# Second image of a linear-attention layer: fewer filter taps on TensorE, output projections placed between its filter sets, and denominators placed ahead of the last key-value product

## The chip, the cores and the metric

The kernel runs on one core of one Trainium2 chip. The metric is the device time of one launch in microseconds. Before the change the median of three runs is 846.25 us (844.39 to 847.61).

The engines are named as in the profile: PE is TensorE (matrix products), PEld its loads of weights, DVE is VectorE, ACT is ScalarE, POOL is GpSimd, SP issues transfers. All data of this layer is float32.

## What is computed

Four layers are applied in turn to x of shape (2, 256, 32, 32), each as `x = x + layer(groupnorm(x))`. The change is in the third, a linear attention with a local branch. Its reference, cut to what matters (B = 2 images, N = 1024 pixels, 768 channels of q, k and v):

```python
qkv = einsum('bchw,oc->bohw', x, w_qkv)                 # 768 channels
y = conv(qkv, w_dw, 5x5, padding 2, one filter per channel)
y = conv(y, w_pw, 1x1, groups of 8 channels)
mqkv = concatenate([qkv, y], axis=1).reshape(B, -1, 24, N)   # heads of 8 q, 8 k, 8 v
q, k = relu(mqkv[:, :, :8]), relu(mqkv[:, :, 8:16])
v = pad(mqkv[:, :, 16:], one more row of ones)
vk = einsum('bhdn,bhen->bhde', v, k)
out = einsum('bhde,bhen->bhdn', vk, q)
out = out[:, :, :-1] / (out[:, :, -1:] + 1e-15)
out = einsum('bchw,oc->bohw', out.reshape(B, -1, H, W), w_proj)
out = batchnorm(out)
```

So there are two sources: qkv itself (source 0) and the filtered y, the "local" branch (source 1). Each has its own keys, values and queries, and both go into the projection.

## The kernel before

**Tiles.** The 768 channels lie in six tiles t of 128: 0 and 2 are keys, 1 and 3 values, 4 and 5 queries. A **unit** (t, b) is a tile of one image, 128 x 1024 values. `Y_UNITS` lists the twelve units in the order in which TensorE finishes them. For image 0 that is tiles 0, 2, 4, 5, 1, 3 (units 0 to 5 of the list), for image 1 tiles 0, 2, 4, 1, 3, 5 (units 6 to 11).

**The 25 taps of a filter are shared out.** The first `TENSOR_TAPS[t]` taps of a unit run on TensorE, with matrices that hold the filter weight times the 1x1 weights, so that the sum lands in its final place. One tap of one unit is a **set**: four matmuls of 64 x 512 in the four corners of the array (`local_set`, L1031). The other taps are summed elsewhere: for tiles 0, 2, 4 and 5 by VectorE, one `scalar_tensor_tensor` of 128 x 1024 per tap with its sum in PSUM banks 6 and 7 (`filter_tap`, L402 for the first, L406 for the rest); for tiles 1 and 3 ScalarE makes the product of each tap (`tap_products`, L1773) in one of four buffers, and GpSimd adds it (L2003 the first, L2006 the rest). `pool_taps` lists these, 19 per unit and 76 in all. TensorE then adds that sum, multiplied by the 1x1 weights, to its own (`local_rest`, four matmuls, L1048), and ScalarE copies the finished unit out (`copy_local`, L1815 to L1819), after which its two banks are free. Units use banks 2, 3 and banks 4, 5 in turn, so the first set of a unit waits until the unit two before it is copied out. `REST_WITHIN` says inside which unit, and before which of its taps, the rest of the unit before is placed; None means that it stands in the written order.

**Keys times values.** For a block n of 128 pixels TensorE transposes keys and values (`key_value_step`, L960), ScalarE copies them out (L1799), and TensorE multiplies them (`key_value_product`, L970). Blocks 0 to 15 are source 0, 16 to 23 source 1 of image 0, 24 to 31 source 1 of image 1. From block 16 on all transposes go through one bank, so each step waits for the copy of the one before. VectorE masks the sum to the heads (`mask_products`, L1422), TensorE multiplies the projection into it (`merge_projection`, L992), ScalarE copies the merged matrix (L1830).

**Queries and output.** TensorE sums the denominators (`denominators`, L983), VectorE inverts them (`invert_denominators`, L1431 and L1432), TensorE spreads the inverses over the channels (`spread_pair`, L1013), VectorE scales the queries (`weigh_queries`, L1438). `project(i, ks)` (L1059) is one block of 128 x 512 of the output: i = 0 to 3 are image 0, 4 to 7 image 1; ks 0 and 1 are source 0, ks 2 and 3 source 1. VectorE adds each block to x (`update_x2`, L1448) and takes moments for the next group normalisation (L1167).

**What sets the order.** Each engine runs its program in order; the interleaving is written out by hand. On TensorE it is the sequence of calls from L1085 on. On VectorE a counter `done` runs over the filter taps, and tables place the other steps after a given tap: `MASK_AT`, `INVERT_AT`, `WEIGH_QUERIES_AT`, `UPDATE_AT`. On ScalarE `PRODUCTS_BEFORE[n]` is the number of tap products made before unit n is copied out. VectorE's units are (0,0), (2,0), (4,0), (5,0), (0,1), (2,1), (4,1), (5,1), with 17 taps each before the change, so taps 102 to 118 are unit (4,1) and 119 to 135 unit (5,1).

Of the kernel before, what the change touches and what calls it, by code (L numbers as in the profile page):

```python
# [37 lines left out]
WT = 8  # L38
TILES = B * WT
# [6 lines left out]
K5 = 25  # L46
TENSOR_TAPS = [8, 6, 8, 6, 8, 8]

HALF = P // 2
QUARTERS = [(0, 0, 0), (1, 0, 1), (0, 1, 1), (1, 1, 0)]  # L50
Y_UNITS = [(t, 0) for t in (0, 2, 4, 5, 1, 3)] + [(t, 1) for t in (0, 2, 4, 1, 3, 5)]
REST_WITHIN = [None, 5, 5, 5, 1, 3, 1, 5, 5, 1, 4, None]
SETS_WITH_KV, SETS_PER_PAIR = 8, 6
WEIGH_AT, WEIGH_LOCAL_AT = 18, 42
MASK_AT = [56, 102]
INVERT_AT = [57, 84]
WEIGH_QUERIES_AT = [61, 66, 71, 76, 87, 90]
UPDATE_AT = [107, 111, 126, 129]
PRODUCTS_BEFORE = [31, 36, 41, 44, 50, 54, 70, 74, 76, 76, 76, 76]

# [49 lines left out]
def mixer_kernel(nc, x_in, out, w, xpad_dram, general_dram):  # L110
    cv_at, cv_n = channel_columns()
    with ExitStack() as ctx:
# [202 lines left out]
        for t in range(QKV_TILES):  # L315
            pwt.append(words(o, TENSOR_TAPS[t] * HALF).rearrange("p (a m) -> p a m", m=HALF))
            o += TENSOR_TAPS[t] * HALF
        projw = words(o, 1024).rearrange("p (k c) -> p k c", k=4); o += 1024
# [29 lines left out]
        def den_bank(part):  # L348
            return 0 if part else 1

# [5 lines left out]

        sets_before = [sum(TENSOR_TAPS[t] for t, b in Y_UNITS[:n]) for n in range(len(Y_UNITS) + 1)]

# [24 lines left out]

        pool_taps = [(t, a, b) for b in range(B) for a in range(TENSOR_TAPS[POOL_TILES[0]], K5) for t in POOL_TILES]
        early_tmp = [local[0][4], local[0][5], spare_tmp]
# [12 lines left out]
        def filter_tap(eng, t, b, a):  # L398

            wt = col("dw2_w", t * K5 + a)  # L400
            if a == TENSOR_TAPS[t]:
                return eng.tensor_scalar(filter_acc, tap_view(t, a, b), wt, None, ALU.mult)  # L402
            dst = filter_acc
            if a == K5 - 1:
                dst = local[b][t].rearrange("p (y x) -> p y x", y=H)
            return eng.scalar_tensor_tensor(dst, tap_view(t, a, b), wt, filter_acc, ALU.mult, ALU.add)  # L406
# [274 lines left out]
        def _(pe):  # L681
# [420 lines left out]
            for i in range(2):  # L1102
                project(i, range(4))
                sets = local_sets(sets, sets + 1)
            sets = local_sets(sets, sets_before[11])
            local_rest(10)
            for i in (2, 3):
                project(i, range(4))

            sets = local_sets(sets, sets + 3)  # L1110
            pe.wait_ge(s_yqe, 11)
            pe.wait_ge(s_x_new, 20)
            for n in range(TILES + WT, 2 * TILES):
                key_value_step(n)
                if sets < sets_before[12]:
                    sets = local_sets(sets, sets + 1)
                if n > TILES + WT:
                    key_value_product(n - 1)
                if n == 2 * TILES - 3:
                    local_rest(11)  # L1120
            key_value_product(2 * TILES - 1)
            merge_projection(3)
            for i in (4, 5):
                project(i, (0, 1))
            pe.wait_ge(s_yqe, 12)
            pe.wait_ge(s_mgc, 4)
            denominators(2)
            for i in (6, 7):
                project(i, (0, 1))
            spread_pair(12)  # L1130
            spread_pair(14)
# [28 lines left out]
        def _(dve):  # L1160
# [294 lines left out]
            for u, (t, b) in enumerate(DVE_UNITS):  # L1455
                dve.wait_ge(s_qp, CHUNKS * Q_ORDER.index(t) + 2 * (b + 1))
                for tap in range(TENSOR_TAPS[t], K5):
                    if tap > TENSOR_TAPS[t]:
                        me.upto(tap_n)
                    elif u:  # L1460
                        dve.wait_ge(s_dwd, u)
# [79 lines left out]
        def _(act):  # L1541
# [305 lines left out]
            for n in range(7, 11):  # L1847
                tap_products(PRODUCTS_BEFORE[n])
                copy_local(n)
            copy_turned(TILES + WT, 2 * TILES, 76)  # L1850
            copy_merged(3)
# [38 lines left out]
        def _(pool):  # L1890
# [84 lines left out]
            def tap_matrices(t):  # L1975
                taps = TENSOR_TAPS[t]
                return g.tensor_tensor(pwt[t], pwm[:, t, :].unsqueeze(1).to_broadcast([P, taps, HALF]),
                                       col("dw2_w", t * K5, taps).unsqueeze(2).to_broadcast([P, taps, HALF]), ALU.mult)
# [12 lines left out]
            for n, (t, tap, b) in enumerate(pool_taps):  # L1991
                if tap == TENSOR_TAPS[t] and b == 1:
                    pool.wait_ge(s_tr, TILES)
                if n == WEIGH_AT:
                    pool.wait_ge(s_qf, CHUNKS * (Q_ORDER.index(2) + 1))
                    denominator_weights(0, 0, 2)
                if n == WEIGH_LOCAL_AT:
                    pool.wait_ge(s_yqe, 2)
                    denominator_weights(1, 0, 1)
                pool.wait_ge(s_tp, n + 1)  # L2000
                dst = local[b][t]
                if tap == TENSOR_TAPS[t]:
                    g.tensor_copy(dst, tap_tmp(n)).then_inc(s_ta, 1)  # L2003
                else:
                    pool.wait_ge(s_ta, n - 1)
                    g.tensor_tensor(dst, dst, tap_tmp(n), ALU.add).then_inc(s_ta, 1)  # L2006
# [161 lines left out]
```

## Time and profile before

| | us |
|---|---|
| median of three runs | 846.25 |
| the profiled execution | 846.58 |
| its span, first to last instruction | 844.9 |
| third layer's filters and attention, first VectorE tap to last projection | 544.8 to 789.0 |
| of it, from image 0's projections on | 703.3 to 789.0 |
| PE busy, share of the span | 692.0 (82%) |
| DVE busy | 559.9 (66%) |
| ACT busy | 330.7 (39%) |
| POOL busy | 350.5 (41%) |

The profiled execution is 0.33 us above the median, and 1.7 us of it lie outside the span. The timelines quoted below have one row per run of like instructions: start in us from the span's start, duration, engine, line, operation, shapes, number of instructions, and in brackets how long the engine had been idle and for what. One fp32 matmul of the code shows as two MATMUL records, so a set is x8 and one `project` over four ks is x8. In a table of stretches PEclk is the granted clock of TensorE as a share of its full 2.4 GHz; 0.50 is 1.2 GHz.

### The profile page before, as it was taken

The numbers are of one execution on the slowest core, as the hardware profiler recorded it, in microseconds if no ns is written. First come the engines' busy times: TensorE is split into PE (matmuls) and PEld (weight loads), VectorE is DVE, ScalarE is ACT, GpSimd is POOL, SyncE is SP. The second block draws the span as 40 slices with busy tenths as digits, with TensorE's granted clock in tenths as the row PEclk, the third lists the DMA queues.
The fourth block names the chain that finished last, engine by engine and source line by source line (L and its number), as shares of the span: only waits on it lengthen the run. The fifth ranks groups of instructions, "written<-read, shape, count | busy, mean of one in ns | idle before, by whom it ended". The sixth has DMA issues, their size and how long they took to land.

```text
span 844.9 us, 8797 instructions
## 1 busy us (share of the span) xinstructions
PE 692.0 (82%) x3446; PEld 376.2 (45%) x3446; DVE 559.9 (66%) x616; ACT 330.7 (39%) x454; POOL 350.5 (41%) x196
## 2 busy tenths in 40 slices
PE   1959346987986799999799999597999988898666
PEld 0656145777983465443211555243533343243222
DVE  6895878993957335301235323699999998762797
ACT  3603680002000433001344111379889867421433
POOL 5620029998650532000000000519999979400260
PEclk9989769999999899999978999798999999899789
DMA  5059100085102713900216300200000000000002
GB/s 177 0 80 153 17 2 1 1 118 97 24 1 73 251 74 144 402 27 1 100 65 209 125 1 0 80 0 1 1 1 1 1 1 2 1 1 1 13 0 99
DMA packets 37622, 49.51 MB, mean 59 GB/s; under 512 B 2628, under 2 KB 25988, under 8 KB 36252
## 3 DMA queue, kind: packets, MB, share of 16 engines
q1 hardware_dynamic: 37580, 48.94, 21.3%
q8 instruction: 27, 0.44, 0.2%
q14 instruction: 15, 0.12, 0.1%
HBM read 28.19 MB, written 10.49 MB: 46 GB/s over the span
## 4 chain that ended last, share of the span: by engine, by line
PE 50%; DVE 29%; POOL 8%; issue 5%; ACT 4%; DMA 3%; SPq 0%; POOLq 0%; DVEq 0%; ACTq 0%
DVE psum L406 14%; PE psum L822 8%; PE psum L760 6%; PE psum L932 3%; PE psum L793 3%; POOL arena L1930 3%; PE psum L1031 3%; PE psum L736 3%; POOL arena L1933 3%; PE psum L1059 2%; PE psum L918 2%; PE psum L896 2%; DVE psum L436 2%; PE psum L1154 2%; PE psum L695 2%
## 5 line engine op out<-in xcount | busy, mean ns | idle before, releaser
L406 DVE SCALAR_TENSOR_TENSOR psum<-arena,psum 128x1024 f32<-128x1024 f32 x120 | 154.6, 1289 | 3.8
L2006 POOL TENSOR_TENSOR arena<-arena 128x1024 f32<-128x1024 f32 x72 | 143.6, 2029 | 11.0 <-ACT arena L1773 10.4
L760 PE MATMUL psum<-arena 128*128 128x128 f32 x800 | 93.6, 277 | 12.9 <-DVE arena L477 8.9
L760 PEld LDWEIGHTS psum<-arena 128*128 128x128 f32 x800 | 88.6, 142 | 17.8 <-DVE arena L477 10.9
L477 DVE TENSOR_TENSOR arena<-arena,psum 128x2048 f32<-128x2048 f32 x38 | 83.9, 2285 | 17.4 <-ACT psum L1673 13.5
L1031 PE MATMUL psum<-arena 64*64 64x512 f32 x704 | 90.0, 627 | 0.9 <-ACT arena L1817 0.9
L1773 ACT ACTIVATE arena<-arena 128x1024 f32<-128x1024 f32 x76 | 87.2, 1179 | 4.5 <-POOL arena L2006 4.5
L1965 POOL MEMSET arena<- 128x864 f32 x1 | 0.8, 836 | 197.1 <-DVE arena L1403 197.1
L822 PE MATMUL psum<-arena 128*128 128x512 f32 x144 | 63.8, 602 | 0.0
L477 POOL TENSOR_TENSOR arena<-arena 128x2048 f32<-128x2048 f32 x12 | 43.6, 3651 | 13.5 <-PE psum L760 13.4
L747 PE MATMUL psum<-arena 128*128 128x128 f32 x162 | 21.4, 294 | 31.2 <-DVE arena L1312 31.2
L947 PE MATMUL psum<-arena 128*128 128x512 f32 x96 | 43.0, 610 | 4.3 <-ACT arena L1569 4.3
L1031 PEld LDWEIGHTS psum<-arena 64*64 64x64 f32 x704 | 24.9, 136 | 47.3 <-issue 47.3
L822 PEld LDWEIGHTS psum<-arena 128*128 128x128 f32 x144 | 27.0, 188 | 36.6 <-issue 36.6
L1357 DVE TENSOR_REDUCE arena<-arena 128x16 f32<-128x496 f32 (+1 forms) x12 | 7.4, 669 | 50.8 <-ACT arena L1722 50.8
L1336 DVE TENSOR_TENSOR arena<-arena 128x512 f32<-128x512 f32 x16 | 12.1, 756 | 38.5 <-ACT arena L1710 38.3
L1669 ACT ACTIVATE arena<-psum 128x512 f32<-128x512 f32 x8 | 4.4, 600 | 83.7 <-PE psum L760 83.7
L747 PEld LDWEIGHTS psum<-arena 128*128 128x128 f32 x162 | 20.4, 208 | 32.7 <-issue 26.4
L1407 DVE TENSOR_TENSOR arena<-arena,psum 128x512 f32<-128x512 f32 x16 | 11.0, 687 | 35.6 <-PE psum L871 35.6
L1059 PE MATMUL psum<-arena 128*128 128x512 f32 x64 | 30.2, 621 | 2.2 <-ACT arena L1830 1.4
L1799 ACT ACTIVATE arena<-psum 128x512 f32<-128x512 f32 x32 | 19.1, 597 | 31.6 <-PE psum L960 31.5
L947 PEld LDWEIGHTS psum<-arena 128*128 128x128 f32 x96 | 18.8, 197 | 27.8 <-issue 22.9
(229 smaller groups left out, 1278.3 us busy)
## 6 DMA issues: line engine op xcount, KB each, us to landing
arena<-fc_w_dram SPq DMA_DIRECT2D x10, 1024.0 KB, 11.9
bounce<-arena SPq DMA_DIRECT2D x32, 256.0 KB, 2.0
arena<-bounce SPq DMA_DIRECT2D x32, 256.0 KB, 5.3
arena<-arena SPq DMA_DIRECT2D x16, 480.0 KB
arena<-x_dram SPq DMA_DIRECT2D x4, 512.0 KB, 5.0
out_dram<-arena SPq DMA_DIRECT2D x4, 512.0 KB, 2.6
arena<-sp_w_dram SPq DMA_DIRECT2D x1, 1152.0 KB
arena<-arena SPq DMA_DIRECT2D x8, 140.0 KB
```

What stands on the lines that cost most here:

```text
L406: return eng.scalar_tensor_tensor(dst, tap_view(t, a, b), wt, filter_acc, ALU.mult, ALU.add)
L477: return eng.tensor_tensor(prods[n % NB].rearrange("p (x g c) -> p x g c", g=GH, c=CG), shifted(hf, j, i), weight, ALU.mult)
L736: m = pe.matmul(psum[:, t % 8, 0:NOM], g1cm[:, k, t, :], omw[:, k], start=(k == 0), stop=(k == 1))
L747: m = pe.matmul(psum[:, bank, at * XG:(at + 1) * XG], ident, wk[n % 2][:, (3 * i + j) * XG:(3 * i + j + 1) * XG], start=(bank not in opene ...
L760: m = pe.matmul(psum[:, 4 * hf + xx // 4, xx % 4 * P:(xx % 4 + 1) * P], prods[n % NB][:, xx * P:(xx + 1) * P], ident, start=(first and xx ...
L793: m = pe.matmul(psum[:, i % 4, :], Zc1[:, 2 * k + b, t::WT], pw1w[:, k], start=(k == 0), stop=(k == 1))
L822: m = pe.matmul(psum[:, c, :], sp1w[:, k, tap], Z[:, 2 * k + b, y0:y0 + 16, PAD - 1 + dx:PAD - 1 + dx + W], start=(k == 0 and tap == 0), s ...
L947: m = pe.matmul(psum[:, i % 4, :], qkvw[:, k, t * P:(t + 1) * P], z2[:, k, c * BANK:(c + 1) * BANK], start=(k == 0), stop=(k == 1))
L1031: pe.matmul(psum[y_rows(to), y_banks(n)[half], :], pwt[t][rows, tap, :], padq[rows, t, b, y0:y0 + 16, dx:dx + W], start=(tap == 0), stop=F ...
L1059: m = pe.matmul(psum[:, proj_bank(i), :], merged[:, src, b, gr, mh * P:(mh + 1) * P], queries(src, b, gr)[:, c * BANK:(c + 1) * BANK], sta ...
L1773: a.activation(tap_tmp(n).rearrange("p (y x) -> p y x", y=H), tap_view(t, tap, b), ACT.Copy, scale=col("dw2_w", t * K5 + tap)).then_inc(s_ ...
L2006: g.tensor_tensor(dst, dst, tap_tmp(n), ALU.add).then_inc(s_ta, 1)
```

## The change

Image 1 gets its own numbers of taps on TensorE: `[8, 4, 8, 4, 8, 5]` in place of `[8, 6, 8, 6, 8, 8]`. That is 37 sets in place of 44. Tiles 1 and 3 of image 1 have 21 taps instead of 19 on ScalarE and GpSimd (80 in all instead of 76), and tile 5 of image 1 has 20 instead of 17 on VectorE (139 taps in all instead of 136). Image 0 and the buffers for the matrices keep their sizes. The tables of VectorE and ScalarE are set anew, two projections of image 0 move in between the sets, the rest of unit 9 moves behind the last set of unit 10, and the end of the layer is reordered. The denominators of image 1 move from bank 0 to bank 7.

```diff
-TENSOR_TAPS = [8, 6, 8, 6, 8, 8]
+TENSOR_TAPS = [[8, 6, 8, 6, 8, 8], [8, 4, 8, 4, 8, 5]]
-REST_WITHIN = [None, 5, 5, 5, 1, 3, 1, 5, 5, 1, 4, None]
+REST_WITHIN = [None, 5, 5, 5, 1, 3, 1, 5, 5, 1, None, None]
-MASK_AT = [56, 102]
+MASK_AT = [56, 105]
-UPDATE_AT = [107, 111, 126, 129]
-PRODUCTS_BEFORE = [31, 36, 41, 44, 50, 54, 70, 74, 76, 76, 76, 76]
+UPDATE_AT = [110, 114, 121, 127]
+PRODUCTS_BEFORE = [31, 36, 41, 44, 50, 54, 70, 74, 78, 80, 80, 80]
...
         def den_bank(part):
-            return 0 if part else 1
+            return (1, 0, 7)[part]
...
             for i in range(2):
                 project(i, range(4))
                 sets = local_sets(sets, sets + 1)
+            sets = local_sets(sets, sets_before[9])
+            project(2, range(4))
+            sets = local_sets(sets, sets_before[10])
+            project(3, range(4))
             sets = local_sets(sets, sets_before[11])
+            local_rest(9)
             local_rest(10)
-            for i in (2, 3):
-                project(i, range(4))
-
-            sets = local_sets(sets, sets + 3)
+
+            sets = local_sets(sets, sets + 2)
             pe.wait_ge(s_yqe, 11)
             pe.wait_ge(s_x_new, 20)
...
+            pe.wait_ge(s_yqe, 12)
+            denominators(2)
             key_value_product(2 * TILES - 1)
-            merge_projection(3)
             for i in (4, 5):
                 project(i, (0, 1))
-            pe.wait_ge(s_yqe, 12)
+            merge_projection(3)
+            project(6, (0, 1))
+            spread_pair(12)
+            project(7, (0, 1))
             pe.wait_ge(s_mgc, 4)
-            denominators(2)
-            for i in (6, 7):
-                project(i, (0, 1))
-            spread_pair(12)
             spread_pair(14)
```

The first place is TensorE from the second projection of image 0 to the first transposes of image 1's local keys and values. L1031 is sets (x4 is one set), L1048 rests, L1059 projections, L960 transposes. Before:

```order
L1059 MATMUL psum<-arena 128x512 x4
L1031 MATMUL psum<-arena 64x512 x20
L1048 MATMUL psum<-arena 64x512 x4
L1031 MATMUL psum<-arena 64x512 x16
L1048 MATMUL psum<-arena 64x512 x4
L1031 MATMUL psum<-arena 64x512 x36
L1048 MATMUL psum<-arena 64x512 x4
L1031 MATMUL psum<-arena 64x512 x8
L1048 MATMUL psum<-arena 64x512 x4
L1059 MATMUL psum<-arena 128x512 x8
L1031 MATMUL psum<-arena 64x512 x12
L960 MATMUL psum<-arena 128x128 x4
```

The same stretch in the changed kernel:

```order
L1031 MATMUL psum<-arena 64x512 x20
L1048 MATMUL psum<-arena 64x512 x4
L1031 MATMUL psum<-arena 64x512 x12
L1059 MATMUL psum<-arena 128x512 x4
L1031 MATMUL psum<-arena 64x512 x4
L1048 MATMUL psum<-arena 64x512 x4
L1031 MATMUL psum<-arena 64x512 x12
L1059 MATMUL psum<-arena 128x512 x4
L1031 MATMUL psum<-arena 64x512 x16
L1048 MATMUL psum<-arena 64x512 x8
L1031 MATMUL psum<-arena 64x512 x8
L960 MATMUL psum<-arena 128x128 x4
```

One projection now stands ahead of the rest of unit 8 (the second L1048) and one behind it, the rests of units 9 and 10 stand together (x8), and 18 sets stand between the projection and the transposes where there were 23.

The second place is the end of the layer on TensorE, from the last transposes to the last projections: L970 are products of keys and values, L983 the denominators, L992 the merge, L1013 the spreading. Before:

```order
L960 MATMUL psum<-arena 128x128 x4
L970 MATMUL psum<-arena 128x128 x4
L992 MATMUL psum<-arena 128x256 x2
L1059 MATMUL psum<-arena 128x512 x4
L983 MATMUL psum<-arena 32x512 x4
L1059 MATMUL psum<-arena 128x512 x4
L1013 MATMUL psum<-arena 128x512 x4
L1059 MATMUL psum<-arena 128x512 x8
```

And in the changed kernel:

```order
L960 MATMUL psum<-arena 128x128 x4
L970 MATMUL psum<-arena 128x128 x2
L983 MATMUL psum<-arena 32x512 x4
L970 MATMUL psum<-arena 128x128 x2
L1059 MATMUL psum<-arena 128x512 x4
L992 MATMUL psum<-arena 128x256 x2
L1059 MATMUL psum<-arena 128x512 x2
L1013 MATMUL psum<-arena 128x512 x2
L1059 MATMUL psum<-arena 128x512 x2
L1013 MATMUL psum<-arena 128x512 x2
L1059 MATMUL psum<-arena 128x512 x8
```

The denominators moved ahead of the last product, the merge behind two half projections, and the other two half projections stand ahead of and between the spreads.

The third place is VectorE at unit (4,1), from its first tap on. L1422 (L1425 in the changed kernel) is the mask, L1448 (L1451) an update of x:

```order
 L402 TENSOR_SCALAR psum<-arena 128x1024
-L1422 TENSOR_TENSOR arena<-psum,arena 128x256
-L406 SCALAR_TENSOR_TENSOR psum<-arena,psum 128x1024 x5
-L1448 SCALAR_TENSOR_TENSOR arena<-psum,arena 128x512
+L406 SCALAR_TENSOR_TENSOR psum<-arena,psum 128x1024 x3
+L1425 TENSOR_TENSOR arena<-psum,arena 128x256
+L406 SCALAR_TENSOR_TENSOR psum<-arena,psum 128x1024 x5
+L1451 SCALAR_TENSOR_TENSOR arena<-psum,arena 128x512
 L406 SCALAR_TENSOR_TENSOR psum<-arena,psum 128x1024 x4
```

Three taps of the unit moved ahead of the mask; the distances from the mask to the first two updates, five and four taps, stayed.

## Rows read from the trace of the kernel before

**Rows 1.** The page's chain that ended last, shares of the span by line:
```profile
DVE psum L406 14%; PE psum L822 8%; PE psum L760 6%; PE psum L932 3%; PE psum L793 3%; POOL arena L1930 3%; PE psum L1031 3%; PE psum L736 3%; POOL arena L1933 3%; PE psum L1059 2%; PE psum L918 2%; PE psum L896 2%; DVE psum L436 2%; PE psum L1154 2%; PE psum L695 2%
```
**Rows 2.** Timeline of DVE, units (4,1) and (5,1) (start, duration, what, idle before):
```profile
700.25 0.42 DVE L1422 TENSOR_TENSOR arena<-psum,arena 128x256 f32<-128x256 f32 x1 [4.26 <-PE psum L970]
...
714.96 7.90 DVE L406 SCALAR_TENSOR_TENSOR psum<-arena,psum 128x1024 f32<-128x1024 f32 x6
722.89 1.28 DVE L406 SCALAR_TENSOR_TENSOR arena<-arena,psum 128x1024 f32<-128x1024 f32 x1
...
743.02 0.75 DVE L1448 SCALAR_TENSOR_TENSOR arena<-psum,arena 128x512 f32<-128x512 f32 x1 [8.18 <-PE psum L1059]
...
756.12 1.28 DVE L406 SCALAR_TENSOR_TENSOR arena<-arena,psum 128x1024 f32<-128x1024 f32 x1
```
**Rows 3.** Timeline of PE up to the key-value steps of image 1:
```profile
680.25 0.63 PE L960 MATMUL psum<-arena 128*128 128x128 f32 x4 [2.06 <-issue]
...
711.62 4.61 PE L1031 MATMUL psum<-arena 64*64 64x512 f32 x40
716.05 1.04 PE L1048 MATMUL psum<-arena 64*64 64x512 f32 x8
716.90 2.80 PE L1031 MATMUL psum<-arena 64*64 64x512 f32 x24
720.18 1.11 PE L1031 MATMUL psum<-arena 64*64 64x512 f32 x8 [0.48 <-ACT arena L1817]
724.23 1.98 PE L1048 MATMUL psum<-arena 64*64 64x512 f32 x8 [2.94 <-DVE arena L406]
...
738.29 1.06 PE L1048 MATMUL psum<-arena 64*64 64x512 f32 x8
```
**Rows 4.** Stretches: length, busy of PE, PEld, DVE, ACT, POOL, PEclk, DMA, GB/s:
```profile
680.00:700.70 20.70, 18.39 (x136) 9.35 (x136) 15.98 (x15) 18.06 (x27) 17.63 (x9) 1.00 0.00 1
...
724.20:729.70 5.50, 5.47 (x28) 1.78 (x32) 5.28 (x5) 2.37 (x4) 2.51 (x5) 0.50 0.02 3
...
767.30:770.60 3.30, 3.30 (x6) 1.69 (x5) 0.00 (x0) 0.60 (x1) 0.00 (x0) 0.50 0.02 5
```
**Rows 5.** Timeline of POOL, the last 13 tap additions:
```profile
700.72 25.45 POOL L2006 TENSOR_TENSOR arena<-arena 128x1024 f32<-128x1024 f32 x13 [0.43 <-ACT arena L1773]
```
**Rows 6.** Timeline of ACT, tap products and copies of finished units:
```profile
720.06 2.24 ACT L1773 ACTIVATE arena<-arena 128x1024 f32<-128x1024 f32 x2
...
739.40 2.40 ACT L1815 ACTIVATE arena<-psum 64x512 f32<-64x512 f32 x4 [0.21 <-PE psum L1048]
```
**Rows 7.** Timeline of PE, key-value steps of image 1 and the end:
```profile
749.13 0.66 PE L960 MATMUL psum<-arena 128*128 128x128 f32 x4
...
760.25 1.09 PE L1048 MATMUL psum<-arena 64*64 64x512 f32 x8
761.27 0.66 PE L960 MATMUL psum<-arena 128*128 128x128 f32 x4
...
762.61 0.66 PE L960 MATMUL psum<-arena 128*128 128x128 f32 x4 [0.24 <-ACT arena L1799]
...
765.51 0.71 PE L970 MATMUL psum<-arena 128*128 128x128 f32 x4 [1.80 <-ACT arena L1799]
766.74 1.62 PE L992 MATMUL psum<-arena 128*128 128x256 f32 x4 [0.52 <-DVE arena L1422]
768.15 4.85 PE L1059 MATMUL psum<-arena 128*128 128x512 f32 x8
772.93 1.91 PE L983 MATMUL psum<-arena 128*32 128x512 f32 x8
774.77 3.70 PE L1059 MATMUL psum<-arena 128*128 128x512 f32 x8
779.05 1.99 PE L1013 MATMUL psum<-arena 32*128 32x512 f32 x8 [0.57 <-DVE arena L1432]
781.81 7.14 PE L1059 MATMUL psum<-arena 128*128 128x512 f32 x16 [0.78 <-DVE arena L1438]
```

More of the change, by code:

```diff
@@ L315, in mixer_kernel @@
         for t in range(QKV_TILES):
-            pwt.append(words(o, TENSOR_TAPS[t] * HALF).rearrange("p (a m) -> p a m", m=HALF))
-            o += TENSOR_TAPS[t] * HALF
+            pwt.append(words(o, TENSOR_TAPS[0][t] * HALF).rearrange("p (a m) -> p a m", m=HALF))
+            o += TENSOR_TAPS[0][t] * HALF
         projw = words(o, 1024).rearrange("p (k c) -> p k c", k=4); o += 1024
@@ L355, in vk_sum @@
             return psum[:, 1, 0:2 * P] if src else psum[:, 0, 2 * P * b:2 * P * (b + 1)]
-        sets_before = [sum(TENSOR_TAPS[t] for t, b in Y_UNITS[:n]) for n in range(len(Y_UNITS) + 1)]
+        sets_before = [sum(TENSOR_TAPS[b][t] for t, b in Y_UNITS[:n]) for n in range(len(Y_UNITS) + 1)]
         def y_banks(n):
@@ L381, in mixer_kernel @@
         DVE_UNITS = [(t, b) for b in range(B) for t in DVE_TILES]
-        pool_taps = [(t, a, b) for b in range(B) for a in range(TENSOR_TAPS[POOL_TILES[0]], K5) for t in POOL_TILES]
+        pool_taps = [(t, a, b) for b in range(B) for a in range(TENSOR_TAPS[b][POOL_TILES[0]], K5) for t in POOL_TILES]
         early_tmp = [local[0][4], local[0][5], spare_tmp]
@@ L400, in filter_tap @@
             wt = col("dw2_w", t * K5 + a)
-            if a == TENSOR_TAPS[t]:
+            if a == TENSOR_TAPS[b][t]:
                 return eng.tensor_scalar(filter_acc, tap_view(t, a, b), wt, None, ALU.mult)
@@ L1456, in _ @@
                 dve.wait_ge(s_qp, CHUNKS * Q_ORDER.index(t) + 2 * (b + 1))
-                for tap in range(TENSOR_TAPS[t], K5):
-                    if tap > TENSOR_TAPS[t]:
+                for tap in range(TENSOR_TAPS[b][t], K5):
+                    if tap > TENSOR_TAPS[b][t]:
                         me.upto(tap_n)
@@ L1849, in _ @@
                 copy_local(n)
-            copy_turned(TILES + WT, 2 * TILES, 76)
+            copy_turned(TILES + WT, 2 * TILES, len(pool_taps))
             copy_merged(3)
@@ L1975, in tap_matrices @@
             def tap_matrices(t):
-                taps = TENSOR_TAPS[t]
+                taps = TENSOR_TAPS[0][t]
                 return g.tensor_tensor(pwt[t], pwm[:, t, :].unsqueeze(1).to_broadcast([P, taps, HALF]),
@@ L1991, in _ @@
             for n, (t, tap, b) in enumerate(pool_taps):
-                if tap == TENSOR_TAPS[t] and b == 1:
+                if tap == TENSOR_TAPS[b][t] and b == 1:
                     pool.wait_ge(s_tr, TILES)
@@ L2001, in _ @@
                 dst = local[b][t]
-                if tap == TENSOR_TAPS[t]:
+                if tap == TENSOR_TAPS[b][t]:
                     g.tensor_copy(dst, tap_tmp(n)).then_inc(s_ta, 1)
```

## The prediction

> **What bounds the kernel now.** I read four things in this order. First the page's chain of work that ended last: VectorE's filter taps (L406) are its largest line with 14% of the span, and only 2 to 3% each are TensorE's sets and projections [rows 1]. In the stretch that the change touches, the timelines say more. The second view is VectorE's timeline. It is packed with taps until 695.99, waits 4.26 us for the last product of image 0's local keys and values, is packed again until 734.8, waits 8.18 us for a projection, and ends unit (5,1) at 757.4 [rows 2]. The third is TensorE's. It waits 0.48 and 2.94 us inside unit 9, the second time for VectorE's unit (4,1) [rows 3], and that wait costs more than itself: the granted clock is 0.50 from 724.2 to 729.7 [rows 4]. From 724.23 on it has no wait until 762 [rows 3, 7]. So VectorE sets the pace up to 724 and TensorE from there to 765. The fourth view is the end: TensorE and VectorE take turns (product, mask, merge, denominators, inverse, spread, scaling), and image 1's last projections start at 781.81 [rows 7]. What follows, 63.1 us to the end of the span, has the same instructions before and after, and I take it as shifted.
>
> **VectorE.** One tap takes (722.89 - 714.96) / 6 = 1.322 us [rows 2]. Three taps of unit (4,1) now stand ahead of the mask: 3 x 1.322 = 3.97, inside the wait of 4.26. They end at 699.96, and the mask still runs at 700.25. The cover is 0.29 us; if it is gone, each us is a us for everything behind. Updates 0 and 1 keep their distances, so VectorE stands at 714.96 as before. Four taps then end unit (4,1) at 720.2, where it was 724.2. After that 3 taps, update 2, 6 taps, update 3 with two moments, and 11 taps: 20 x 1.322 = 26.4, and 2.7 for the two updates and the moments (two updates at some 0.7, moments 1.2). Unit (5,1) ends at 720.2 + 26.4 + 2.7 = 749.4, and update 3 at 733.5. The three added taps thus fill the old wait, and the 8.18 us wait is gone as long as projections 2 and 3 come before VectorE asks for them (724.2 and 732.8).
>
> **GpSimd and ScalarE.** Thirteen additions take 25.45 us, 1.96 each, and the last ended at 726.2 [rows 5]. Four more: 734.0. ScalarE was free at 720.06 and has four products to make in place of two [rows 6], at 1.1 each; they fit into its waits. The copy of unit 8 stands before the last two, and by the times below the first of those two is made by 728.8, while GpSimd wants it at 726.2 + 2 x 1.96 = 730.1. Cost on the path nothing, as long as TensorE asks for the rest of unit 9 after 734.0.
>
> **TensorE up to the transposes.** Prices at full clock: a set (716.05 - 711.62) / 5 = 0.89, a rest 716.90 - 716.05 = 0.85 [rows 3], a projection 7.14 / 2 = 3.57 [rows 7]. Until 716.90 nothing changes. Then:
> three sets and project 2: 716.9 + 2.7 + 3.6 = 723.2 (its wait for update 0 is over since 708);
> one set, then the rest of unit 8: 724.1 to 725.0. VectorE ended the unit at 720.2, so the wait of 2.94 us is gone, and with it the idle stretch that came before the fall of the clock;
> three sets, project 3, four sets: 725.0 + 2.7 + 3.6 + 3.6 = 734.9;
> rests of units 9 and 10: GpSimd is done since 734.0, so they run to 736.6.
> Now a wait that was not there. The first set of unit 11 needs unit 9 copied out. A copy starts 1.11 us after its rest starts (738.29 to 739.40) and takes 2.40 [rows 3, 6]: 734.9 + 1.1 + 2.4 = 738.4. TensorE idles 1.8 us. Two sets end at 740.2, and the copy of unit 10 ends at 738.6 + 2.4 = 741.0: 0.8 more. The transposes start at **741.0** where it was 749.13: **8.1 earlier**. The account of it: five sets less, 4.4; the two waits, 3.4; 5.5 us at half clock, 2.75; less 2.6 of new waits; 8.0.
>
> **Key-value steps.** From the first transposes to the rest of unit 11 it was 760.25 - 749.13 = 11.1 us with five sets in between [rows 7]. Now three. A step without a set can't be shorter than transposes, copy, next transposes: 762.61 - 761.27 = 1.34, where a step with one takes some 2.1. So 2 x 0.78 = **1.6 less**, and the rest of unit 11 is reached at 741.0 + 9.5 = 750.5. VectorE's 749.4 is 1.1 ahead of it.
>
> **The end.** Call that moment R. Before, from R = 760.25: the copy of unit 11 ended at R + 4.6, the last product stood at R + 5.3, the projections of ks 2 and 3 at R + 21.6 [rows 7]. Now the denominators start at R + 4.6 and take 1.84 (774.77 - 772.93); the last product is done at R + 7.1, the mask at R + 7.6, the inverse at about R + 11.7 (0.7 and 3.4, between 774.8 and 779.05). Meanwhile TensorE does half projections 4 and 5 (3.6, to R + 10.7), the merge (1.0 to 1.4, to R + 11.8), half projection 6 (1.8), the first spread (1.99 / 2 = 1.0), half projection 7 (1.8) and reaches the second spread at R + 16.4. From the first spread's start to the last projections it was 781.81 - 779.05 = 2.8, from the second's 1.0 less, 1.8. So R + 18.2, **3.4 less**. The 1.5 us or so that half clock cost between 767.3 and 770.6 [rows 4] is part of that: the old gap before it, 1.80 and 0.52 us around the last product, shrinks to about 1.2 us.
>
> **Sum.** 8.1 + 1.6 + 3.4 = 13.1. The profiled execution took 846.58, so 833.5 for such a one. It stands 0.33 above the median, so the median after is 833.15, say **833.1**.
>
> **A rule against it.** TensorE gets two new waits 1.9 us apart, 1.8 and 0.8 us long. In the trace, waits of 1.80 and 0.52 within 3 us were followed by 1.2 GHz from 767.3 to 770.6, while one of 2.06 us before 680.25 was followed by none: the clock stays 1.00 from 680 to 700.7 [rows 3, 4, 7]. The rows thus bear out both. The Trainium skill, page "TensorE: Matmul & The Clock Gate", section "A second HAM failure mode: psum-queue depth-cycling", says that short pauses between groups of matmuls that cycle through PSUM banks are enough to make the clock swing between its two levels. The first of the two places agrees with it and the second doesn't. As a mechanism of this kernel it is rival B.
>
> **Rivals.**
> A, the sum above: 833.1, chance 0.55.
> B, the clock falls around 740 after the new waits. It would then be low for 3.3 to 5.5 us of busy TensorE, as at 767 and 724 [rows 4], which costs half of that, 1.7 to 2.8, less the slack of the steps that wait for ScalarE's copy anyway. 835 to 836, chance 0.22.
> C, the margins are too thin: VectorE's unit (5,1), GpSimd's last addition and the mask have 1.1, 0.9 and 0.3 us. If each resource comes 1 to 3 us later than I add up, for instance because ScalarE makes the last two products late (their margin is 1.3 us), or if the end takes the old 21.6 us because the inverse, not TensorE, ends last, the gain shrinks to 7 to 11 us: 835 to 839. Against it: all pitches are from the same stretch. Chance 0.13.
> D, better than the sum: the new waits for copies, 2.6 us, are shorter than I add up, and so is the end behind the last projections. 829 to 832, chance 0.05.
> E, slower. GpSimd and ScalarE lock: the copy of unit 8 stands on ScalarE ahead of products 78 and 79, and it waits for a rest that waits for VectorE. If VectorE ended unit (4,1) x us later than 720.2, TensorE has 724.1 - 720.2 = 3.9 us of cover; from there on every us goes to the rest of unit 9, then to the copies, the transposes, everything. The gain is used up at x of about 3.9 + 13.1 = 17. Against it: VectorE's taps vary by hundredths, and nothing that it waits for moved later. At 851, with x = 22, chance 0.03.
> F, the change does nothing: the projections only swap places and the end is set by something I don't see in these rows, such as a longer stretch behind 781.81. 845 to 848, chance 0.02.
>
> **How the numbers follow.** The forecast is A's 833.1. For 8 in 10 I take A, B, most of C, and the scatter of the runs before, 844.39 to 847.61, so about 1.6 each way: 829.5 to 838.5. Half a per cent, 4.2 us, is about what a measurement of this kernel can tell from no change. Faster by more than that: A to D, 0.95. Within: F, 0.02. Slower: E, 0.03.
>
> **What would show it.** In the profile after: the mask still at 700.3 with no idle time before it to speak of; no wait of TensorE for VectorE before the rest of unit 8, and clock 1.00 from 720 to 735; a wait of about 1.8 us for a copy before unit 11's first set; transposes of image 1 at 741; the rest of unit 11 at 750.5 without a wait; denominators at 755; the last four half projections at 768.7; the end of the span at 831.8. A wait of TensorE for GpSimd before the rests of units 9 and 10 would say C, PEclk of 0.50 between 738 and 746 B. The prediction is wrong if the stretch behind the last projections is not just shifted, or if the transposes do not start before 745.

## The result, and the profile after

The changed kernel takes 835.1 us (median of 4 runs, 832.3 to 836.7) where the kernel before took 845.3 beside it: a ratio of 0.988, 95% interval 0.983 to 0.992. Timed twice more it gave 832.7 and 832.3, with ratios of 0.986 (0.982 to 0.990) and 0.985 (0.982 to 0.989). Over all runs the medians are 832.7 (16 runs) and 846.0 (49 runs), 13.3 us apart; but the runs are of several sets, and set by set the gain by these ratios is 10.5, 11.8 and 12.5 us. The forecast was 833.1, 13.1 below the median of 846.25 before.

The profiled execution after has a span of 835.0 us. The timelines below have the same columns as those of before. The lines of code behind TensorE's key-value steps are 3 higher than before (the mask is L1425, an update L1451, the copies L1818 to L1822); L1059 and those ahead of it have kept their numbers. Since the same point of the program lies at different times in different executions, times are best counted from one event. I use VectorE's **mask** of image 0's local keys and values. VectorE, where [rows 2] stood:

```profile
697.94 3.94 DVE L406 SCALAR_TENSOR_TENSOR psum<-arena,psum 128x1024 f32<-128x1024 f32 x3
702.14 0.42 DVE L1425 TENSOR_TENSOR arena<-psum,arena 128x256 f32<-128x256 f32 x1 [0.26 <-PE psum L970]
...
726.03 0.75 DVE L1451 SCALAR_TENSOR_TENSOR arena<-psum,arena 128x512 f32<-128x512 f32 x1
...
749.72 1.28 DVE L406 SCALAR_TENSOR_TENSOR arena<-arena,psum 128x1024 f32<-128x1024 f32 x1
759.65 0.42 DVE L1425 TENSOR_TENSOR arena<-psum,arena 128x256 f32<-128x256 f32 x1 [8.64 <-PE psum L970]
```

The wait of 4.26 us ahead of the mask is 0.26; three taps fill it. The wait of 8.18 us for projection 2 is gone. TensorE, where [rows 3] and the head of [rows 7] stood:

```profile
718.78 2.81 PE L1031 MATMUL psum<-arena 64*64 64x512 f32 x24
721.51 3.70 PE L1059 MATMUL psum<-arena 128*128 128x512 f32 x8
725.15 1.11 PE L1031 MATMUL psum<-arena 64*64 64x512 f32 x8
726.08 1.03 PE L1048 MATMUL psum<-arena 64*64 64x512 f32 x8
...
736.84 1.89 PE L1048 MATMUL psum<-arena 64*64 64x512 f32 x16
740.49 1.97 PE L1031 MATMUL psum<-arena 64*64 64x512 f32 x16 [1.76 <-ACT arena L1818]
742.83 0.66 PE L960 MATMUL psum<-arena 128*128 128x128 f32 x4 [0.37 <-ACT arena L1818]
```

There is no wait for VectorE ahead of the rest of unit 8 (726.08), and the new one for unit 9's copy is there (740.49). The clock, in two stretches (columns as in [rows 4]), where [rows 4] showed 0.50:

```profile
724.00:735.00 11.00, 11.00 (x67) 3.66 (x69) 10.79 (x10) 6.93 (x9) 11.00 (x7) 1.00 0.01 1
...
738.00:746.00 8.00, 5.88 (x48) 1.85 (x40) 7.79 (x7) 5.87 (x10) 0.00 (x0) 1.00 0.00 0
```

GpSimd, as [rows 5]:

```profile
702.59 33.25 POOL L2009 TENSOR_TENSOR arena<-arena 128x1024 f32<-128x1024 f32 x17 [0.39 <-ACT arena L1776]
```

ScalarE, as [rows 6]: the last two tap products, and the copies of units 9 and 10 back to back:

```profile
729.61 2.25 ACT L1776 ACTIVATE arena<-arena 128x1024 f32<-128x1024 f32 x2
...
737.95 4.83 ACT L1818 ACTIVATE arena<-psum 64x512 f32<-64x512 f32 x8 [6.09 <-PE psum L1048]
```

And the end of the layer on TensorE, as the rest of [rows 7]:

```profile
752.41 1.09 PE L1048 MATMUL psum<-arena 64*64 64x512 f32 x8
...
757.05 1.91 PE L983 MATMUL psum<-arena 128*32 128x512 f32 x8 [1.18 <-ACT arena L1822]
...
768.53 1.13 PE L1013 MATMUL psum<-arena 32*128 32x512 f32 x4
770.44 7.14 PE L1059 MATMUL psum<-arena 128*128 128x512 f32 x16 [0.78 <-DVE arena L1441]
```

From the mask to the last four half projections it is 770.44 - 702.14 = 68.30 us, where it was 81.56: **13.26 us gained in this stretch**. The span fell by 9.9 only. The other 3.4 lie outside: the mask itself came 1.89 later (702.14, before 700.25), and behind the last projections it is 835.0 - 770.44 = 64.6 where it was 63.1. The code behind the last projections is unchanged, and so is that of the layers ahead of this one. So the question for the experiments was whether the 13.26 are solid, which parts of the change they belong to, and what the other 3.4 are.

### The profile page after: what moved, and what is told of

It reads as the page before. It is cut to its first block, busy times and chain, and to the rows that moved or that the text cites. A ratio compares the mean times of both kernels' runs of the same rounds, so it can differ in the third digit from the quotient of the medians.

```text
span 835.0 us, 8704 instructions
## 1 busy us (share of the span) xinstructions
PE 684.3 (82%) x3390; PEld 374.0 (45%) x3390; DVE 563.7 (68%) x619; ACT 335.0 (40%) x458; POOL 357.3 (43%) x200
## 4 chain that ended last, share of the span: by engine, by line
PE 52%; DVE 25%; POOL 8%; ACT 7%; issue 3%; DMA 3%; SPq 0%; DVEq 0%; POOLq 0%; ACTq 0%
DVE psum L406 12%; PE psum L822 8%; PE psum L760 7%; PE psum L1031 3%; PE psum L1059 3%; PE psum L932 3%; PE psum L793 3%; POOL arena L1933 3%; PE psum L736 3%; POOL arena L1936 3%; PE psum L918 2%; PE psum L896 2%; PE psum L1157 2%; DVE psum L436 2%; PE psum L840 2%
## 5 line engine op out<-in xcount | busy, mean ns | idle before, releaser
L406 DVE SCALAR_TENSOR_TENSOR psum<-arena,psum 128x1024 f32<-128x1024 f32 x123 | 158.5, 1288 | 3.9
L2009 POOL TENSOR_TENSOR arena<-arena 128x1024 f32<-128x1024 f32 x76 | 151.2, 2027 | 11.2 <-ACT arena L1776 10.9
L1776 ACT ACTIVATE arena<-arena 128x1024 f32<-128x1024 f32 x80 | 91.7, 1180 | 5.0 <-POOL arena L2009 4.9
L1031 PE MATMUL psum<-arena 64*64 64x512 f32 x648 | 82.4, 622 | 2.2 <-ACT arena L1818 1.8
L822 PE MATMUL psum<-arena 128*128 128x512 f32 x144 | 63.8, 602 | 0.0
L947 PE MATMUL psum<-arena 128*128 128x512 f32 x96 | 43.1, 612 | 4.3 <-ACT arena L1572 4.3
L1031 PEld LDWEIGHTS psum<-arena 64*64 64x64 f32 x648 | 22.4, 134 | 44.5 <-issue 44.5
L1672 ACT ACTIVATE arena<-psum 128x512 f32<-128x512 f32 x8 | 4.3, 600 | 85.4 <-PE psum L760 85.4
L1059 PE MATMUL psum<-arena 128*128 128x512 f32 x64 | 29.4, 602 | 2.2 <-ACT arena L1833 1.4
L932 PE MATMUL psum<-arena 128*128 128x512 f32 x64 | 28.6, 598 | 2.8 <-ACT arena L1762 2.8
```

What stands on the lines that cost most here:

```text
L822: m = pe.matmul(psum[:, c, :], sp1w[:, k, tap], Z[:, 2 * k + b, y0:y0 + 16, PAD - 1 + dx:PAD - 1 + dx + W], start=(k == 0 and tap == 0), s ...
L932: m = pe.matmul(psum[:, 4 + j % 4, :], pw2w[:, k, mh * P:(mh + 1) * P], OT[b][:, k, t - 3:t + 1, :], start=(k == 0), stop=(k == KM - 1))
L947: m = pe.matmul(psum[:, i % 4, :], qkvw[:, k, t * P:(t + 1) * P], z2[:, k, c * BANK:(c + 1) * BANK], start=(k == 0), stop=(k == 1))
L1031: pe.matmul(psum[y_rows(to), y_banks(n)[half], :], pwt[t][rows, tap, :], padq[rows, t, b, y0:y0 + 16, dx:dx + W], start=(tap == 0), stop=F ...
L1059: m = pe.matmul(psum[:, proj_bank(i), :], merged[:, src, b, gr, mh * P:(mh + 1) * P], queries(src, b, gr)[:, c * BANK:(c + 1) * BANK], sta ...
L1776: a.activation(tap_tmp(n).rearrange("p (y x) -> p y x", y=H), tap_view(t, tap, b), ACT.Copy, scale=col("dw2_w", t * K5 + tap)).then_inc(s_ ...
```

## The experiments

M stands for that stretch, mask to last half projections. A total's median moves by some us between sets of runs; M, read from one profile, turned out to repeat to 0.01 in the three profiles of the changed kernel. The kernel before has one profile; the one with only the end changed repeats it up to the rest of unit 11 (59.99 us after the mask, and 60.00 before).

**The changed kernel again, twice.**

> The changed kernel once more. M is the time from VectorE's mask of image 0's local keys and values (one L1422 or L1425) to the start of the last four half projections (L1059 x16): 81.56 us before, 68.30 in the first profile after. Theory 1 (the stage gained what the sum says, 13.1, and the rest of the difference lies outside it): M is 68.3 within 0.2 again, while the stretches ahead of the mask and behind the last projections vary by 1 to 2 us from run to run. Theory 2 (the stage itself varies, and 68.3 was a lucky run): M is off by over 1 us. Total near 835.

> The changed kernel a third time, beside the other two on the same chip. Theory 1: M = 68.3 within 0.1. Total 833 to 835; ratio to the kernel before 0.984 to 0.988. What lies ahead of the first tap and behind the last projections differs from run to run with the places where the clock falls.

M was 68.30 and 68.29, though the mask stood at 694.41 and 696.75. Every inner distance repeated too (first transposes 40.69 and 40.68 after the mask, rest of unit 11 50.27 and 50.26). Theory 1 holds.

**The old order at the end, and the new order alone.** The first kernel puts the change's end, with the bank of the denominators, in the kernel before; the second takes it out of the changed kernel. The first:

```diff
-            return 0 if part else 1
+            return (1, 0, 7)[part]
...
+            pe.wait_ge(s_yqe, 12)
+            denominators(2)
             key_value_product(2 * TILES - 1)
-            merge_projection(3)
             for i in (4, 5):
                 project(i, (0, 1))
-            pe.wait_ge(s_yqe, 12)
+            merge_projection(3)
+            project(6, (0, 1))
+            spread_pair(12)
+            project(7, (0, 1))
             pe.wait_ge(s_mgc, 4)
-            denominators(2)
-            for i in (6, 7):
-                project(i, (0, 1))
-            spread_pair(12)
             spread_pair(14)
```

> The kernel before with the new order at the end of the layer alone (denominators of image 1 ahead of the last product, merge and half projections moved, denominators in bank 7); taps and projections 2 and 3 as before. Theory 1, terms add up: from the rest of unit 11 to the last half projections 18.0 us in place of 21.6, so M = 81.6 - 3.5 = 78.1, total 3.5 below before. Theory 2, the order at the end pays only together with the rest (the inverse or the mask ends last): M stays at 81.6 or falls by under 1.

> The changed kernel with the old order at the end of the layer. Theory 1: M = 68.3 + 3.5 = 71.8. If the wait before the last product is followed by a low clock as before, that is in the 3.5. Theory 2: M stays within 1 us of 68.3.

Measured: M = 78.03 with the new end alone, 71.83 with it undone, so 3.53 both ways; from the rest of unit 11 on 18.04 and 21.57. Totals: ratio 0.996 (0.993 to 0.999) and 0.992 (0.988 to 0.995). The term adds up, and does not depend on the rest. About half of it is clock. In the kernel with the end undone, TensorE's merge and first two half projections are

```profile
757.86 1.99 PE L992 MATMUL psum<-arena 128*128 128x256 f32 x4 [0.52 <-DVE arena L1425]
759.65 4.47 PE L1059 MATMUL psum<-arena 128*128 128x512 f32 x8
```

at a granted clock of 0.51 from 757.9 to 761.3; in the changed kernel the same instructions take 1.03 and 3.60 at 1.00. That is 1.8 us. How the rest divides between the denominators, the merge and the half projections, no run separates.

**The new order with the old tap counts.**

```diff
-TENSOR_TAPS = [[8, 6, 8, 6, 8, 8], [8, 4, 8, 4, 8, 5]]
+TENSOR_TAPS = [[8, 6, 8, 6, 8, 8], [8, 6, 8, 6, 8, 8]]
-MASK_AT = [56, 105]
+MASK_AT = [56, 102]
-UPDATE_AT = [110, 114, 121, 127]
-PRODUCTS_BEFORE = [31, 36, 41, 44, 50, 54, 70, 74, 78, 80, 80, 80]
+UPDATE_AT = [107, 111, 118, 124]
+PRODUCTS_BEFORE = [31, 36, 41, 44, 50, 54, 70, 74, 76, 76, 76, 76]
-            sets = local_sets(sets, sets + 2)
+            sets = local_sets(sets, sets + 3)
```

> The new order with the old numbers of taps (six and eight for image 1 too; mask after tap 102, updates after 107, 111, 118, 124, three sets of unit 11 ahead of the transposes). Theory 1: TensorE no longer waits for VectorE before the rest of unit 8, the clock stays at 1.00, transposes of image 1 44.3 us after the mask, rest of unit 11 11.1 later, 18.0 to the end: M = 73.5, so the order is worth 8 us and the tap counts 5. Theory 2, the tap counts carry the gain: M of 78 or more.

M = 73.89: the order, both places and the end's 3.5 together, is worth 7.7 of the 13.3, the tap counts 5.6 (0.8 for each of the seven sets). Its ratio is 0.990 (0.984 to 0.995). TensorE has no wait for VectorE to speak of before the rest of unit 8 here either, and the clock stays at 1.00 from 715 to 770. VectorE's last tap of the unit and TensorE's rest:

```profile
723.41 1.28 DVE L406 SCALAR_TENSOR_TENSOR arena<-arena,psum 128x1024 f32<-128x1024 f32 x1
...
724.75 1.09 PE L1048 MATMUL psum<-arena 64*64 64x512 f32 x8
```

So for that wait the place of projection 2 is enough, but only just: the tap ends at 724.69, 0.06 us ahead of the rest. The three taps ahead of the mask add 4.0 us of cover there, and make room for VectorE's three more taps.

**The clock alone.** In the kernel before, three matmuls whose result nobody reads are put into TensorE's wait for VectorE:

```diff
                 if tap == REST_WITHIN[n]:
+                    if n == 9:
+                        pe.wait_ge(s_x_new, 17)
+                        for _ in range(3):
+                            pe.matmul(psum[:, 0, :], ident, flat[4][:, 0:BANK], start=True, stop=True)
                     local_rest(n - 1)
```

> The kernel before with three more matmuls of 128 x 512 (their result in bank 0 is overwritten unread) in TensorE's wait for VectorE's unit (4,1), some 2.6 us of the 2.9. It tests the price of the clock alone. Theory 1: the granted clock stays at 1.00 from 720 to 735, and the transposes of image 1 start 2.7 us earlier: M = 78.8. Theory 2, the low clock is due to something else or costs nothing: clock 0.50 as before, M = 81.6 or more.

TensorE's timeline (its lines from the sets on are 4 higher than before):

```profile
716.72 2.84 PE L1030 MATMUL psum<-arena 128*128 128x512 f32 x6
719.73 1.09 PE L1052 MATMUL psum<-arena 64*64 64x512 f32 x8 [0.17 <-DVE arena L406]
720.65 8.04 PE L1035 MATMUL psum<-arena 64*64 64x512 f32 x72
```

And the clock in the stretch that had been low (columns as in [rows 4]):

```profile
719.70:729.40 9.70, 9.67 (x92) 3.36 (x96) 9.37 (x8) 2.36 (x4) 2.51 (x5) 1.00 0.01 2
```

The rest of unit 8 starts 23.98 us after the mask as in the kernel before, so only what follows it has changed. Nine sets take 8.04 us and the rest 1.09; they took 9.89 and 1.98 in the kernel before. The transposes start 46.19 after the mask instead of 48.88, and M is 78.73: **2.8 us for work that only keeps TensorE busy**. The total's ratio is 0.997 (0.994 to 1.000), which by itself is barely clear of no change. The price of the wait for VectorE was thus its own 2.9 and 2.7 of clock.

**VectorE's margin.** In the changed kernel the mask goes back:

```diff
-MASK_AT = [56, 105]
+MASK_AT = [56, 102]
```

> The changed kernel with the mask back after tap 102; the updates stay after taps 110, 114, 121, 127. VectorE then idles some 4 us ahead of the mask and has all later taps 3.97 us later. Theory 1 (margins of the profile after): unit (5,1) had ended 1.4 us before TensorE asked for it, so only 4.0 - 1.4 = 2.6 of it reach the end: M = 70.9, with a wait of TensorE for VectorE before the rest of unit 11. Theory 2, VectorE sets the pace throughout: M = 72.3. Theory 3, VectorE is fully hidden: M = 68.3.

TensorE's timeline around the rest of unit 11:

```profile
749.35 1.61 PE L1048 MATMUL psum<-arena 64*64 64x512 f32 x8 [2.47 <-DVE arena L406]
750.89 1.11 PE L960 MATMUL psum<-arena 128*128 128x128 f32 x4
...
752.69 0.88 PE L960 MATMUL psum<-arena 128*128 128x128 f32 x4
```

M = 71.85. The rest of unit 11 came 52.84 after the mask, 2.57 later than 50.27, as theory 1 had it (2.6). The other 0.98 lie behind it: the wait of 2.47 us was followed by a low clock (0.56 from 749.3 to 753.2), and the rest took 1.61 instead of 1.09. The margin of VectorE was 1.4 us, and this wait cost more than its length. The total, with a ratio of 0.988 (0.984 to 0.992), can't be told from the changed kernel's.

**GpSimd's share, one tap more and one less for each of its two units.**

```diff
-TENSOR_TAPS = [[8, 6, 8, 6, 8, 8], [8, 4, 8, 4, 8, 5]]
+TENSOR_TAPS = [[8, 6, 8, 6, 8, 8], [8, 3, 8, 3, 8, 5]]
-PRODUCTS_BEFORE = [31, 36, 41, 44, 50, 54, 70, 74, 78, 80, 80, 80]
+PRODUCTS_BEFORE = [31, 36, 41, 44, 50, 54, 70, 74, 78, 82, 82, 82]
```

> The changed kernel with 3 taps on TensorE for tiles 1 and 3 of image 1 in place of 4: two sets less, two additions more (82). Theory 1: GpSimd had ended 0.9 us before TensorE asked; it now ends 3.9 later and TensorE asks 1.8 earlier, so the rest of unit 9 comes 3.0 later and M = 71.3; TensorE idles 4.7 us there, and if the clock falls after it, up to 2.7 more, 74. Theory 2, TensorE alone sets the pace: M = 66.5.

> The changed kernel with 5 taps on TensorE for tiles 1 and 3 of image 1: two sets more, two additions less (78). Theory 1: TensorE sets the pace there, so two sets more cost 1.8: M = 70.1. Theory 2, GpSimd or the copies set it: M within 0.5 of 68.3 or below.

With 82 additions TensorE waits for GpSimd, and then runs at half clock:

```profile
739.19 3.69 PE L1048 MATMUL psum<-arena 64*64 64x512 f32 x16 [4.65 <-POOL arena L2009]
743.79 3.69 PE L1031 MATMUL psum<-arena 64*64 64x512 f32 x16 [0.91 <-ACT arena L1818]
```

```profile
739.20:747.50 8.30, 7.39 (x33) 1.76 (x34) 8.09 (x7) 4.74 (x8) 0.48 (x3) 0.50 0.00 0
```

The two rests take 3.69 us where they took 1.89, the two sets 3.69 where they took 1.97 (the last row is the stretch, columns as in [rows 4]). M = 73.86, the upper of the two cases of theory 1. With 78 additions M = 70.09, 1.79 more for two sets (expected 1.8). By M the share of four taps is the best of the three; the totals (ratios of 0.989 and 0.987 with 82 and 78 additions) do not separate them from the changed kernel.

**Two more moves.** The margins point to two places: TensorE's wait of 1.76 us for the copy of unit 9, which exists because GpSimd ends both its units at the same time, and the waits of 1.18 and 0.78 at the end.

```diff
+        pool_taps = pool_taps[:-6] + sorted(pool_taps[-6:], key=lambda p: POOL_TILES.index(p[0]))
+        added = {(t, b): n + 1 for n, (t, a, b) in enumerate(pool_taps)}
...
-REST_WITHIN = [None, 5, 5, 5, 1, 3, 1, 5, 5, 1, None, None]
+REST_WITHIN = [None, 5, 5, 5, 1, 3, 1, 5, 5, 1, 1, None]
...
-            local_rest(9)
             local_rest(10)
...
-                    pe.wait_ge(s_ta, len([p for p in pool_taps if p[2] <= b]))
+                    pe.wait_ge(s_ta, added[t, b])
...
-                    pool.wait_ge(s_ta, n - 1)
+                    pool.wait_ge(s_ta, max(k + 1 for k in range(n) if pool_taps[k][0] == t))
```

The second kernel adds the end:

```diff
-            pe.wait_ge(s_yqe, 12)
-            denominators(2)
             key_value_product(2 * TILES - 1)
-            for i in (4, 5):
-                project(i, (0, 1))
+            project(4, (0, 1))
+            pe.wait_ge(s_yqe, 12)
+            denominators(2)
+            project(5, (0, 1))
             merge_projection(3)
             project(6, (0, 1))
             spread_pair(12)
-            project(7, (0, 1))
             pe.wait_ge(s_mgc, 4)
             spread_pair(14)
+            project(7, (0, 1))
...
-                    if n == 2 * TILES - 2:
+                    if n == 2 * TILES - 1:
                         copy_local(11)
```

> Move (1) alone. Theory 1: transposes 38.3 us after the mask, 2.4 earlier, but VectorE's unit (5,1) ends at 48.86 and gates the rest of unit 11 at 48.9, so M = 67.0, only 1.3 of the 2.4. Theory 2, TensorE sets the pace alone: M = 65.9.

> The changed kernel with two more moves. (1) GpSimd finishes tile 1 of image 1 three additions before tile 3, so the rest of unit 9 can stand before the second set of unit 10, and its copy is done when TensorE reaches unit 11. (2) At the end ScalarE copies the last turned block before unit 11, and TensorE does the last product, a half projection, the denominators, a half projection, merge, a half projection, both spreads, the last half projection. Theory 1, from the margins: the wait of 1.76 us goes, transposes 38.3 us after the mask; the rest of unit 11 now waits for VectorE at 48.9 (its unit ends at 48.86 as before); the end takes 16.0 in place of 18.0. M = 64.9, 3.4 below the changed kernel. Theory 2, VectorE's chain (mask, inverse 4.1 us, scalings) ends last at the end: M = 66 to 67. Total, if the rest is unchanged, 3 us below the changed kernel.

TensorE in the second kernel (its lines here are 2 higher than in the changed kernel):

```profile
741.77 0.66 PE L962 MATMUL psum<-arena 128*128 128x128 f32 x4 [0.79 <-ACT arena L1819]
...
751.57 1.09 PE L1050 MATMUL psum<-arena 64*64 64x512 f32 x8
...
757.64 1.91 PE L985 MATMUL psum<-arena 128*32 128x512 f32 x8
...
763.98 1.99 PE L1015 MATMUL psum<-arena 32*128 32x512 f32 x8
765.90 8.86 PE L1061 MATMUL psum<-arena 128*128 128x512 f32 x20
```

The first move alone gives M = 66.94 (expected 67.0). The transposes come 39.1 after the mask, 0.8 later than expected since the copy of unit 10 still has to be waited for, but that is hidden: VectorE's unit (5,1), 48.86 after the mask, is what the rest of unit 11, at 48.92, has waited for. Both moves: the rest of unit 11 stands 48.91 after the mask (702.66), and from it to the last projections it is some 16.05 us instead of 18.03, so M is 64.96 (their start lies inside the row of 20; it is set here 2.02 us ahead of VectorE's next update, as in the profile after). Expected was 64.9. The total is 828.4 us (6 runs, ratio 0.980, 0.978 to 0.983), beside 832.3 for the changed kernel on the same chip (0.985, 0.982 to 0.989) and 833.1 for the first move alone (0.985, 0.981 to 0.989). So both moves together give a kernel ahead of both by M. By the medians it is 3.9 us ahead of the changed kernel, but the six runs of each overlap (824.8 to 833.8 and 826.2 to 834.8) and so do the intervals. The first alone shows in M, not in the medians.

**What lies outside M.** No kernel was run for this; the profiles at hand answer it. Behind the last projections TensorE idles for some 7 us, and then the 16 pointwise products of the fourth layer (L1154, in the changed kernel L1157) start at a low clock. Low time after their start against the stretch from the last half projections to the end of the span:

| profile | low clock after their start, us | last half projections to end of span, us |
|---|---|---|
| before | 2.8 | 63.09 |
| new end alone | 3.0 | 63.11 |
| old tap counts | 3.8 | 63.55 |
| after | 6.2 | 64.56 |
| changed kernel again | 6.1 | 64.69 |
| and a third time | 6.1 | 64.56 |

3.4 us more at half clock go with 1.5 us more time, about half. The other seven profiles lie on the same line, from 3.8 us and 63.59 to 6.1 and 64.48. Note that all three profiles of the changed kernel have the long form, while the kernel before has one profile, of the short form: whether the 1.5 us come with the change or by chance is not shown. The row of before:

```profile
822.44 15.38 PE L1154 MATMUL psum<-arena 128*128 128x512 f32 x32 [7.18 <-DVE arena L1512]
```

and that of after:

```profile
810.87 17.05 PE L1157 MATMUL psum<-arena 128*128 128x512 f32 x32 [7.21 <-DVE arena L1515]
```

Ahead of the mask, the first VectorE tap of the third layer stands at 544.77 before, 546.69 after, and between 537.8 and 547.2 over all thirteen profiles, while from it to the mask it is 155.4 to 155.5 in every one. Most of the scatter arises in the second layer, in its loop over the spectrum, between 424 and 470: the loop starts at 423.5 to 425.9 in all profiles, and from its end to the first tap it is 77.3 to 77.6. Stretches of it (columns as in [rows 4]), of the kernel before:

```profile
424.00:430.00 6.00, 6.00 (x18) 0.93 (x18) 2.43 (x4) 1.62 (x2) 0.00 (x0) 0.50 0.11 44
...
461.00:468.00 7.00, 7.00 (x22) 1.70 (x19) 3.00 (x5) 1.79 (x3) 0.00 (x0) 0.58 0.48 185
```

and of the kernel with 78 additions, which was the earliest:

```profile
424.00:430.00 6.00, 6.00 (x36) 1.24 (x36) 3.46 (x6) 3.47 (x6) 0.00 (x0) 1.00 0.22 87
...
454.00:461.00 7.00, 6.13 (x29) 1.87 (x26) 4.61 (x8) 2.39 (x4) 0.00 (x0) 1.00 0.87 333
```

The same loop does half the matmuls in the same time where the clock is 0.50. From its first matmuls (L896) to the next step (L918) it takes 43.4 us in the first, 15.7 of them at a low clock, and 36.7 in the second, with none. The thirteen profiles fall in three groups: no low clock and 36.7 us (two of them), 3.6 to 4.2 us low and 38.4 to 38.6 (four), 15.7 to 16.2 us low and 43.4 to 44.0 (seven). The changed kernel's own three profiles lie one in each. Whether the clock is low there thus differs between executions of unchanged code. Why it is low in some is not tested.

## Why the prediction was right

By its own steps, times counted from the mask (700.25 before):

| step | predicted | measured after |
|---|---|---|
| wait ahead of the mask left | 0.3 | 0.26 |
| VectorE's unit (5,1) ends | 49.1 | 48.86 |
| GpSimd's last addition ends | 33.8 | 33.70 |
| rests of units 9 and 10 start | 34.7 | 34.70 |
| the two new waits of TensorE | 1.8 and 0.8 | 1.76 and 0.37 |
| transposes of image 1 | 40.8 | 40.69 |
| rest of unit 11 | 50.3 | 50.27 |
| from there to the last half projections | 18.2 | 18.03 |
| M | 68.5, 13.1 less | 68.30, 13.26 less |

**VectorE.** Right: three taps went into a wait that already existed. The run with the mask put back shows that they would else have cost 3.6 us, not 4.0, because 1.4 us of margin lay behind, and 1.0 of clock came on top.

**The gain up to the transposes.** Right in the sum, and each part was seen by itself: the filler run prices the clock at 2.7, as the 5.5 us at half clock of [rows 4] had it. The second new wait was sized twice too long (0.8 for 0.37): two sets took 1.97, not 1.8, and began 0.2 later than I had them, while the copies ended where I had them (4.83 for both). It changed the transposes by less than 0.1.

**The key-value steps and the end.** Right: 9.58 us for what had taken 11.12, and 3.53 from the order at the end, which the runs that put it in and took it out confirm both ways. 1.8 of the 3.53 are clock, as the 1.5 or so of the prediction had it.

**Rival B,** the clock falling after the new waits, did not come about: it stayed at 1.00 from 724 to 783. Waits of 1.76 and 0.37 us with two sets between them were followed by no fall (the three profiles of the changed kernel, and the three with the end undone, the mask put back and 78 additions), nor was one of 1.18 before the denominators. Waits of 1.80 and 0.52 with one product between them were followed by one in before, in the kernel with the old end and in the filler kernel, that of 2.47 with the mask put back too. And a single wait of 2.12 to 2.15 us for VectorE's inverse (672.13 after), which is 0.66 in the kernel before (670.20), was followed by one in all three profiles of the changed kernel, there from 673.5 to 677; it is hidden, since the mask stands 155.4 to 155.5 after the first tap either way. The 2.06 of [rows 3] was not. The Trainium skill reports, of a bf16 kernel, that short pauses between groups of matmuls make the clock swing ("TensorE: Matmul & The Clock Gate", section "A second HAM failure mode: psum-queue depth-cycling"). The 1.80 and 0.52 us agree with it, and the 1.76 and 0.37 do not: here it was not enough that there were pauses. What decides, no run shows.

**Rival C,** too thin margins: they were about as thin as said (0.26, 1.0 and 1.4 us measured), and held. The runs that exceed them lost what the step says, and the fall of the clock in addition. **Rival E's** chain needs 17 us of delay; nothing of it was seen.

**What failed** is the step that took what follows 781.81 as shifted, and with it everything ahead of the mask: both were put at nothing. In the first profile 1.9 us came in ahead and 1.5 behind, from where the clock was low in unchanged code, and the end of the span, forecast at 831.8, came at 835.0. By its own last line the prediction counted a stretch behind that is not just shifted as a sign of being wrong, and that sign was seen. The 1.9 ahead is scatter: over the three profiles of the changed kernel the first tap starts at 546.69, 538.96 and 541.30. The 1.5 behind stood in all three. 13.26 less 1.5 is 11.8, beside the three sets' 10.5, 11.8 and 12.5; each of their intervals is some 3 us wide to either side and holds 13.1 too. That the medians over all runs are 13.3 apart, so near the forecast, may then be partly luck. The scatter of three runs (844.4 to 847.6) hinted at it, and I had given it 1.6 us each way; single runs of the kernel before spread from 837.9 to 850.5.

## What to carry to other kernels

Count from an event inside the program, not from its start: a stretch of 68 us that repeats to 0.01 us says more about an edit than medians that wander by 3. Before moving work to an engine, look for a wait that it already has, and for the point where another engine asks for its result; the margin between the two is what the move may cost. A wait of TensorE can cost up to double its length: 2.94 us cost 2.7 more here and 2.47 cost 0.98 more, while 2.06 was followed by no fall. Work that is ready, here a projection, is well placed in it.

## What the runs showed of the hardware that I had not expected

Work without any use made the kernel faster: three dummy matmuls of 0.9 us each, in a wait of 2.9 us, saved 2.8 us of M. And much of the scatter of the whole kernel went with TensorE's granted clock in unchanged code: one loop of the second layer took 36.7 us at full clock and 43.4 with 15.7 us at 1.2 GHz, in executions of the same instructions. The first tap of the third layer moved with it, from 537.8 to 544.8.
